# GATv2 edge attention on one core: score rows spread per head, two heads per maximum, the addition of sums one step later, fading on ScalarE

## The reference, cut to what matters

```python
def _gat_layer(h, src, dst, Wl, bl, Wr, br, att, bias, g, b):   # N=3125, H=4 heads, HD=32
    xl = (h @ Wl + bl).reshape(N, H, HD)
    xr = (h @ Wr + br).reshape(N, H, HD)
    e = jax.nn.leaky_relu(xl[src] + xr[dst], NEG)
    score = jnp.einsum('ehd,hd->eh', e, att)
    m = jax.ops.segment_max(score, dst, num_segments=N)
    ex = jnp.exp(score - m[dst])
    den = jax.ops.segment_sum(ex, dst, num_segments=N)
    out = jax.ops.segment_sum((ex / (den[dst] + 1e-16))[:, :, None] * xl[src], dst, num_segments=N)
    ...                                                          # + bias, layer norm, elu
```

## Times and profile before

| | |
|---|---|
| median of three runs | 9064.03 us |
| profiled execution | 9004.81 us, span 9003.1 us |
| instructions | 154403 |
| busy share of the span | PE 63%, PE weight load 51%, DVE 57%, ACT 31%, POOL 41% |
| granted TensorE clock, mean | 0.86 of full speed |
| DMA | 884.50 MB, 98 GB/s over the span |
| first attention pass, first to last `val` | 5281.1 to 6806.6 us |
| second attention pass | to 8505.4 us |

### The profile page before, as it was taken

The page is one execution under the profiler, slowest core; times in us unless marked ns, Lnnn a source line. Parts: engine busy times, 40 slices in busy tenths (PEclk is TensorE's granted clock), DMA queues, the critical chain, the costliest instruction groups (busy, mean ns, idle before and its releaser), DMA issues. The chain is left out here.

```text
span 9003.1 us, 154403 instructions
## 1 busy us (share of the span) xinstructions
PE 5685.8 (63%) x44934; PEld 4616.3 (51%) x44935; DVE 5133.5 (57%) x12349; ACT 2748.7 (31%) x6113; POOL 3659.2 (41%) x3623
## 2 busy tenths in 40 slices
PE   1111117666677775888888357777773777777666
PEld 1000003655577673555555246666662666666566
DVE  7444444999668673333333456666665666666612
ACT  1000000588557552344333212222221222222210
POOL 2666661234000004555555245555551555555300
PEclk9999999888899897898888677888885888888788
DMA  4111113234324223344446023333352333333555
GB/s 159 44 43 43 46 41 139 86 128 140 111 101 156 98 101 85 112 119 118 116 114 105 15 82 93 95 94 98 96 95 47 93 96 95 94 97 96 64 185 191
DMA packets 662769, 884.50 MB, mean 98 GB/s; under 512 B 304425, under 2 KB 487254, under 8 KB 643668
## 3 DMA queue, kind: packets, MB, share of 16 engines
q1 hardware_dynamic: 553028, 674.48, 23.4%
q0 software_dynamic: 109568, 207.74, 11.6%
HBM read 648.77 MB, written 233.08 MB: 98 GB/s over the span
## 5 line engine op out<-in xcount | busy, mean ns | idle before, releaser
L989 POOL DMA_INDIRECT rows<-head_table,idxb x1760 | 1707.7, 970 | 1614.6 <-issue 484.7
L989 POOL DMA_INDIRECT rows<-source_table,idxb x880 | 844.3, 959 | 1800.8 <-ACT idxb L1009 1157.4
L1702 DVE TENSOR_REDUCE gtop<-ps_top 128x1 f32<-128x512 f32 x1760 | 1208.6, 687 | 382.9 <-remote 207.1
L363 POOL DMA_INDIRECT records<-recb,idxb x784 | 768.2, 980 | 440.4 <-issue 372.0
L1839 PE MATMUL ps_top<-srow,sel 128*128 128x128 bf16 x7040 | 668.4, 251 | 297.6 <-DVE gtop L1702 240.2
L1839 PEld LDWEIGHTS ps_top<-srow,sel 128*128 128x128 bf16 x7040 | 549.4, 115 | 401.2 <-DVE gtop L1702 306.5
L391 PE MATMUL ps_g<-hott 64*128 64x128 bf16 x784 | 59.7, 302 | 989.1 <-DVE prior L456 593.8
L1851 PE MATMUL ps_acc<-val,hot 128*128 128x132 f32 x3520 | 615.4, 324 | 95.1 <-issue 72.4
L787 PE MATMUL ps_cells<-hot 128*128 128x128 bf16 x4608 | 481.3, 248 | 255.1 <-DVE hot L745 122.2
L1096 PE MATMUL ps_acc<-rows,pt 128*128 128x128 f32 x3750 | 517.6, 280 | 135.2 <-DVE pt L1117 120.8
L1851 PEld LDWEIGHTS ps_acc<-val,hot 128*128 128x128 f32 x3520 | 532.6, 226 | 131.7 <-issue 101.2
(11 more groups left out here) (327 smaller groups left out, 12548.1 us busy)
## 6 DMA issues: line engine op xcount, KB each, us to landing
logs<-log_counts SPq DMA_DIRECT2D x75, 1600.0 KB
hot<-one_hots SPq DMA_DIRECT2D x440, 256.0 KB
wt<-edge_weights SPq DMA_DIRECT2D x50, 1600.0 KB
one_hots<-hot SPq DMA_DIRECT2D x220, 256.0 KB
hott<-one_hots_t SPq DMA_DIRECT2D x440, 128.0 KB
edge_weights<-both SPq DMA_DIRECT2D x125, 320.0 KB, 2.8
log_counts<-none SPq DMA_DIRECT2D x125, 320.0 KB, 2.2
records<-blank SPq DMA_DIRECT2D x16, 1870.0 KB
```

The source lines that it names most:

```text
L363: g.indirect_dma_start(out=recs[:, :], out_offset=bass.IndirectOffsetOnAxis(ap=idxb[k][:, t:t + 1], axis=0), in_=recb[k][:, t, :], in_offs ...
L989: g.indirect_dma_start(out=rows[r][:, k, :], out_offset=None, in_=table, in_offset=bass.IndirectOffsetOnAxis(ap=idxb[r][:, k:k + 1], axis= ...
L1702: ve.tensor_reduce(gtop[:, h:h + 1], ps_top[h % TOPS][:, :], AX.X, ALU.max).then_inc(topped, 1)
```

## The change

1. Strips. `parts` becomes 5 strips of 32 columns (4 edge tiles and one for the maxima); a tile's strip holds its own 12 score columns and 16 digit columns. PE transposes 4 strips into 28 partitions x 512 columns instead of one 128x128 block; ACT copies 28x512 instead of 128x128. `srow` is 128x512, set to zero once.
2. Spread and maxima. Each head is one matmul of 512 columns (4 a step for 16). `ps_top` is one tile of four banks; two heads are reduced by one DVE instruction, so 2 of 128x1024 stand for 4 of 128x512. All four come ahead of the sums on PE, so that the sums are PE's last work in a step.
3. The addition of `ps_acc` to `faded` is a new first stage, `tail`, one step later and the first work of DVE's step. The pipeline is 7 deep: 14 block numbers a turn, still 26 turns, one more step.
4. `faded` moves from DVE to ACT, as 4 activations of 128x33 with a scale per partition, behind the `srow` copy.
5. ACT's pipeline gets `c`, so ACT too loads 14 block numbers each turn.
6. `ps_sc` and `ps_node` share one bank, `ps_sn`; the node matmuls go behind the score matmuls on PE, with waits on `summed` and `sc_out`.
7. `mask_tables` builds a `sel` of 128 x (4x128) on 28 partitions: 2 selections for digits' borders become 1, 12 become 3, and 3 of 2048 elements become 3 of 512.

The core of the diff:

```diff
-                    count(g.affine_select(out=sel, in_=sel, compare_op=ALU.is_ge, fill=0.0, base=-64,
-                                          pattern=[[-DIG, TG], [0, HEADS * BN]], channel_multiplier=1))
...
-                        for q in range(TG):
-                            part = c.sel[:, q * HEADS:(q + 1) * HEADS, :].rearrange("p h (a n i) -> p (h a) n i", n=values, i=inner)
...
+                        part = sel.rearrange("p h (a n i) -> p (h a) n i", n=values, i=inner)
...
-        parts = [sb(f"parts{k}", [P, P], BF16) for k in range(2)]
+        parts = [sb(f"parts{k}", [P, TG + 1, STRIP], BF16) for k in range(2)]
-        srow = sb("srow", [P, P], BF16)
+        srow = sb("srow", [P, GE], BF16)
...
+                        tail, sums, weights, merge, maxima, score, _ = stages
+                        if tail:
+                            i, r, b = tail
+                            tg = RING * i + r
+                            ve.wait_ge(agg_done, tg + 1)
+                            ve.wait_ge(faded_ok, tg + 1)
+                            ve.tensor_tensor(c.acc[:, bass.ds(b, 1), 0:HEADS * HW],
+                                             faded[:, :, :].rearrange("p f h -> p (f h)").unsqueeze(1),
+                                             ps_acc[:, 0:HEADS * HW].unsqueeze(1), ALU.add).then_inc(acc_done, 1)
...
-                            ve.tensor_reduce(gtop[:, h:h + 1], ps_top[h % TOPS][:, :], AX.X, ALU.max).then_inc(topped, 1)
+                            ve.tensor_reduce(gtop[:, a * PAIR:(a + 1) * PAIR], ps_top[:, a * PAIR:(a + 1) * PAIR, :], AX.X, ALU.max) \
+                                .then_inc(topped, 1)
...
-                    pipeline(nc, ve, c, 6, step)
+                    pipeline(nc, ve, c, 7, step)
...
-                            act.activation(srow[:, :], ps_srow[:, 0:P], ACT.Copy).then_inc(srow_out, 1)
+                            act.activation(srow[0:USED, :], ps_srow[0:USED, 0:GE], ACT.Copy).then_inc(srow_out, 1)
+                        if sums:
+                            act.wait_ge(p_ready, g + 1)
+                            wait(act, acc_done, g)
+                            for h in range(HEADS):
+                                ins = act.activation(faded[:, :, h], c.acc[:, bass.ds(b, 1), 0:HEADS * HW]
+                                                     .rearrange("p a (f h) -> p (a f) h", h=HEADS)[:, :, h],
+                                                     ACT.Copy, scale=p[k][:, SC + h:SC + h + 1])
+                            ins.then_inc(faded_ok, 1)
...
-                    pipeline(nc, act, None, 6, step)
+                    pipeline(nc, act, c, 7, step)
...
-                            pe.transpose(ps_srow[:, 0:P], parts[mr % 2][:, :], c.identb[:, :]).then_inc(srow_ready, 1)
+                            for q in range(TG):
+                                ins = pe.transpose(ps_srow[0:USED, q * P:(q + 1) * P], parts[mr % 2][:, q, 0:USED], c.identb[:, :])
...
                             wait(pe, sc_out, sg)
+                            wait(pe, summed, sg - 3)
...
+                            pe.wait_ge(lo_out, g + 3)
+                            wait(pe, summed, g)
+                            pe.wait_ge(sc_out, sg if score else NG)
...
-                            spread_scores((0, 1, 2))
+                            for a in range(TURNS):
+                                wait(pe, topped, TURNS * (mg - 1) + (a + 1))
+                                for h in range(a * PAIR, (a + 1) * PAIR):
+                                    ins = pe.matmul(ps_top[:, h, :], c.sel[:, h, :], srow[:, :], start=True, stop=True)
+                                ins.then_inc(tops, 1)
...
-                        if maxima:
-                            spread_scores((3,))
```

More of the change, by code:

```diff
@@ L1575, in gatv2_pass @@
 def gatv2_pass(nc, c, table, att, hots, hotts):
-    TOPS = 3
+    PAIR = 2
+    TURNS = HEADS // PAIR
+    NODE = 64
     with ExitStack() as ctx:
@@ L1603, in gatv2_pass @@
         ps_e = pb("ps_e", [D, 512])
-        ps_sc = pb("ps_sc", [P, 512])
+        ps_sn = pb("ps_sn", [P, 512])
         ps_srow = pb("ps_srow", [P, 1024], BF16)
-        ps_top = [pb(f"ps_top{k}", [BN, 512]) for k in range(TOPS)]
-        ps_node = pb("ps_node", [P, 512])
+        ps_top = pb("ps_top", [BN, HEADS, 512])
         ps_acc = pb("ps_acc", [BN, 512])
@@ L1740, in step @@
                     def step(stages):
-                        sums, weights, merge, maxima, score, edges = stages
+                        _, sums, weights, merge, maxima, score, edges = stages
                         if maxima:
@@ L1752, in step @@
                             wait(act, at_edges, n - 3)
-                            hi, mid = (parts[ck][:, m * CUT:(m + 1) * CUT] for m in range(2))
+                            hi, mid = (parts[ck][:, :, m * HEADS:(m + 1) * HEADS] for m in range(2))
                             if score:
-                                act.activation(parts[ck][:, 64:P], c.digits[:, bass.ds(n, 1), :, :].rearrange("p a q j -> p (a q j)"),
+                                act.activation(parts[ck][:, 0:TG, PARTS * HEADS:USED], c.digits[:, bass.ds(n, 1), :, :].rearrange("p a q j -> p (a q) j"),
                                                ACT.Copy).then_inc(dig_out, 1)
@@ L1759, in step @@
                                 act.wait_ge(newtop, RING * merge[0] + merge[1] + 1)
-                            act.activation(hi, sc[cr][:, :], ACT.Copy).then_inc(hi_out, 1)
+                            act.activation(hi, sc[cr][:, :].rearrange("p (q h) -> p q h", h=HEADS), ACT.Copy).then_inc(hi_out, 1)
                         if weights:
@@ L1770, in step @@
                             act.wait_ge(res_ready, n + 1)
-                            act.activation(mid, res[:, :], ACT.Copy).then_inc(mid_out, 1)
+                            act.activation(mid, res[:, :].rearrange("p (q h) -> p q h", h=HEADS), ACT.Copy).then_inc(mid_out, 1)
                         if edges:
@@ L1786, in step @@
                     def step(stages):
-                        sums, weights, _, maxima, score, edges = stages
+                        _, sums, weights, _, maxima, score, edges = stages
                         if maxima:
@@ L1794, in step @@
                             wait(pe, srow_out, mg)
-                            pe.transpose(ps_srow[:, 0:P], parts[mr % 2][:, :], c.identb[:, :]).then_inc(srow_ready, 1)
+                            for q in range(TG):
+                                ins = pe.transpose(ps_srow[0:USED, q * P:(q + 1) * P], parts[mr % 2][:, q, 0:USED], c.identb[:, :])
+                            ins.then_inc(srow_ready, 1)
+                        if score:
+                            si, sr, _ = score
+                            sg = RING * si + sr
+                            pe.wait_ge(bent_ready, sg + 1)
+                            wait(pe, sc_out, sg)
+                            wait(pe, summed, sg - 3)
+                            for q in range(TG):
+                                ins = pe.matmul(ps_sn[:, q * HEADS:(q + 1) * HEADS], bent[sr % 2][:, q * P:(q + 1) * P],
+                                                att4[:, :], start=True, stop=True)
+                            ins.then_inc(sc_ready, 1)
                         if weights:
@@ L1854, in step @@
                             ins.then_inc(agg_done, 1)
-                        if maxima:
-                            spread_scores((3,))
-                    pipeline(nc, pe, c, 6, step)
+                    pipeline(nc, pe, c, 7, step)
 def gcn_pass(nc, c, weights):
```

92 lines of the change are left out of this document (34 added, 58 removed).

## The result

The changed kernel takes 9698.76 us (9690.18 to 9707.68, four runs) beside 9053.38 us for the kernel before (9036.72 to 9085.63, four runs): a ratio of 1.071, interval 1.067 to 1.074. I had forecast 8928 and a range to 9160; it is 645 us slower. The profiled execution has a span of 9705.9 us, 702.8 more than that of before, and both attention passes together grew by 704: 1874.4 us for the first, where the earlier trace rows had 1525.5. Line 1665 of before is line 1674 of after.

What follows compares the result with a forecast made beforehand. POOL's gather bursts, holding PE's signals, were taken to bound the attention steps. Turns 78, pairs 36, ends 2 and mask tables 20 make 136 us off 9064: 8928, range 8830 to 9000, with rivals 8640 to 9160.

Steps and rivals of the forecast that it cites:

- A usual step gains nothing: 6.47 stays: Attention passes: sums come 0.3 to 0.6 us earlier but are held to the same moment, so a step stays 6.47.
- each maximum: DVE's reductions in attention steps: two of 1.22 us for four of 0.687, 0.31 us a step less.
- DVE's work: DVE in an attention step: 4.63 us less 0.29 and 0.31 gives 4.03, a saving that doesn't show.
- what is held at a burst's end: Attention steps: PE's sums, posted late in POOL's gather burst, are held until 0.92 us behind its end.
- My path from release to the sums: Attention step, from the moment held signals pass until PE posts the sums: 2.9 to 3.2 us, was 3.55.
- (b): More pairs, slower: sums slip through more often, POOL runs two bursts on end; step 6.8 to 7.3, 9150 us, chance 0.18.
- (a): The cadence breaks: sums pass each time, POOL runs burst after burst, 5.1 us a step; 8450 us, chance 0.10.
- (c): Nothing moves: PE's load and transpose keep turns as long, only the mask tables count; 9044 us, chance 0.16.
- Turns: Where one turn of eight attention steps follows another: DVE 1.1 us late for 3.5; 1.5 gained, 78 us in 52 turns.
- Fading: `faded` on ACT in attention steps: four instructions of about 0.219 us, 0.88 together, covered; DVE loses 0.290.
- ACT's whole work: ACT in an attention step: 1.63 us plus 0.32 for the copy and 0.88 for fading, 2.83, covered.
- Mask tables: Building the mask tables: twelve selections become three, POOL is done before DVE, 19.8 us gained once.

Runs made afterwards that it cites:

- b_gather1: Kernel before with one of the four gathers of each group in the attention passes, where signals pass freely: 7707.01 us.
- a_lo_early: Kernel after with `lo` moved ahead of the second paired maximum on DVE, signals held: 9185.48 us, ratio 1.014 to before.
- b_short: Kernel before with PE and DVE loading 8 block numbers a turn for 13, signals held: 8968.11 us, ratio 0.995 to before.
- a_faded_dve: Kernel after with the fading back on DVE and no block numbers loaded on ACT, signals free: 8221.79 us, ratio 1.058 to before.
- a_idx_first: Kernel after with ACT's copy of the next indices moved right behind the `srow` copy, signals free: 8197.59 us, ratio 1.054 to before.
- a_res_first: Kernel after with `res` and `lo` moved ahead of both maxima on DVE, signals free: 7965.96 us, ratio 1.025 to before.
- a_by_head: Kernel after with maxima and spread signals by single heads: 7665.48 and 7660.99 us free (ratio 0.986 to before), 8998.8 us held (0.9997).
- b_gather1_2: Kernel before with one of the four gathers of each group in the attention passes, signals held: 8224.05 us, ratio 0.913 to before.

## Why the prediction was wrong

**The step that failed** is "A usual step gains nothing: 6.47 stays". The usual step became 8.90 us. I priced each maximum as DVE's work, 1.22 for two of 0.69, and found that right. I didn't follow what stands *behind* them in program order. `lo` had 1.37 us of maxima ahead of it and 1.37 behind; after has 2.44 ahead and none behind. Without held signals the step was 4.74 us in before (b_gather1), nearly filled by DVE's own work, and the loop through `lo` became 5.70. I had reckoned DVE's work and PE's, but never the loop that goes through both. DVE's work was off as well: 4.32 us a step (947/219) for my 4.03. Neighbouring instructions overlap by about 0.09 us in the trace (`res` starts at 6330.08 and takes 0.17, the next maximum starts at 6330.16), so each of the three instructions that the change takes from DVE gives back less than its length.

**Where signals are held** more was lost: 2.4 us in a usual step for the 1.0 of the loop. I took for granted that what is held at a burst's end stays the sums. In after the spread leaves PE 3.5 us into the burst, so it is held, and the next burst stands behind maximum, `mid`, `bent` and indices. My path from release to the sums (2.9 to 3.2 us) assumed that transposes, scores and `ps_e` were done ahead of the release, as in the earlier trace rows; that only holds if `lo` came ahead of it. That the place of `lo` is the greater part of it here too is shown by a_lo_early (499 of 626 us); how the rest divides between late indices, PE's clock and the pairs is not.

**Rivals.** (b) had the direction but not the mechanism: it expected sums that slip out early, and a step of 6.8 to 7.3. The trace shows no such pairs in usual steps; POOL waits 4.2 us for indices. (a) and (c) didn't occur.

**Turns.** Forecast: DVE late by 1.1 us for 3.5, 78 us gained. The two figures had different yardsticks: 3.5 was DVE's idle time, which holds the load of block numbers itself (2.95 us, now 3.17), and 1.1 was counted against the next release. The idle time could not fall to 1, and did not:

```profile
6406.83 0.29 DVE L1665 TENSOR_TENSOR acc<-faded,ps_acc 128x132 f32 x1 [3.77 <-issue]
```

In after this costs nothing all the same: around this turn `val` starts at 6394.39, 6407.10 and 6411.50, so the long step and the short one behind it take 17.1 us, less than two usual ones. What a turn costs in the kernel before was sized better by b_short: five numbers less are 1.1 us a turn on DVE, 51 of 59 us.

**Fading.** Taken at 0.219, measured 0.340 each and 1.08 for the four of them that overlap, against my 0.88. The estimate from the Trainium skill, "ScalarE: Activation LUTs", section "What ACT_TABLE_LOAD costs", was 0.31 each less an overlap, nearer than my row. That it is covered was nearly right: moving it is worth about 23 us held, and a_faded_dve is no faster than a_idx_first. ACT's whole work is 2.89 us a step (633/219) for my 2.83.

**Mask tables.** Forecast 19.8 us; DVE is last, as said, and the stage went from 54.3 us (from 5098.87 to the end of the last instruction of the earlier trace rows) to 28.6, 25.7 less. From its start to the first `val` it is 21.1 less, 161.2 us for 182.2. The instruction that ends it in after, whose first began at 5114.84:

```profile
5143.16 0.28 DVE L1565 TENSOR_SCALAR reset<-reset 128x220 f32<-128x220 f32 x1
```

## What to carry to other kernels

In a pipeline whose steps run on several in-order engines, follow the loop through its smallest instruction, not only each engine's sum: fusing two operations lengthens what stands ahead of everything queued between them. Ask of each fused instruction which small result used to leave in the middle of it, and put that result ahead of the last piece. Too early is no better: with all pieces behind it, a_res_first had nothing left to fill the waits for the other engine and was 2.5% slower than before. A change of grain must be tried with that instruction moved as well; here the move alone was worth 499 of 626 us.

## What the runs showed of the hardware

The same kernel took 7772 us in two sets of runs and 9003 to 9058 in the others. In the first case the timelines of a_faded_dve and a_by_head have PE's signals pass beside running gathers; in the second, those posted late in a burst of four indirect gathers passed about 1 us behind its end (0.92 in the earlier trace rows, 1.08 in after).

All of the difference that can be placed lies where indirect gathers run. With one gather of four, the first attention pass takes 1170.6 us free (b_gather1) and 1170.2 held (b_gather1_2), with nothing left between the conditions. Of the 1230 us between them, 713 thus go with three of the four gathers of the attention passes (779 us less held, 66 less free). The same two traces place most of the other 517 in stretches that kept all their gathers: the records' gathers (line 363) take 1005.5 us from first to last start free and 1207.9 held, and the message pass before attention (line 1465) 1170.9 free and 1453.7 held, together 485 us.

What puts a set of runs in the one or the other condition stays open, as does how gathers hold a signal. It is not the chip as the record numbers it: chips 9 and 2 were each met in both. A version chosen in one condition need not be best in the other: single heads gave 0.986 free and 0.9997 held.
